# Graph network on one core: the top-p lists are taken from a scratch tile, and the mean of logits moves behind the register loads

## The reference, cut to what matters

```
for n in range(2):
    q = Xa @ W1.T @ W2.T;  k = Xa @ W3.T
    probs = softmax(q @ k.T)                  # 2048 x 2048
    # keep, row by row, the largest probabilities until their sum reaches 0.9
    A = probs * mask;  A = A / A.sum(-1)
    Xf = R @ Xf                               # R: adjacency with self loops, rows normed
    Xa = A @ Xa
    Z = Z + Xf @ U1[n].T + Xa @ U2[n].T
```

## Time and profile before

| | us |
|---|---|
| median of 3 runs (lowest, highest) | 1009.66 (1006.43, 1011.87) |
| the profiled execution | 1009.86 |
| its span from first to last instruction | 1008.1 |
| PE, DVE, ACT, POOL busy | 800.5, 664.4, 474.4, 69.2 |

### The profile page before, as it was taken

One profiled execution on the slowest core, in us unless ns is written; L12 is line 12 of the kernel. 1 busy time (PEld: TensorE's weight loads), 2 busy tenths in 40 slices (PEclk: granted clock), 3 DMA queues, 4 the chain that ended last, 5 costly groups with the idle time before them and its releaser, 6 DMA issues.

```text
span 1008.1 us, 11952 instructions
## 1 busy us (share of the span) xinstructions
PE 800.5 (79%) x3886; PEld 547.4 (54%) x3886; DVE 664.4 (66%) x2092; ACT 474.4 (47%) x945; POOL 69.2 (7%) x63
## 2 busy tenths in 40 slices
PE   4879984988888837568698688785698899994894
PEld 4844432756666726465375566565295485552342
DVE  5967868488597788832879878768777212235715
ACT  4886334336556483224535846856945141024111
POOL 0020001010000000000000000100001200013001
PEclk9889986988989977879697898989799999997898
DMA  9849502544004000000063400601342719200001
GB/s 332 333 167 429 212 10 84 170 164 136 33 1 168 1 1 2 0 2 1 2 213 120 167 1 1 225 2 53 135 167 85 283 52 413 86 1 0 1 0 42
DMA packets 20219, 108.23 MB, mean 107 GB/s; under 512 B 1824, under 2 KB 8752, under 8 KB 9776
## 3 DMA queue, kind: packets, MB, share of 16 engines
q1 hardware_dynamic: 18752, 106.77, 28.5%
q10 hardware_dynamic: 1392, 0.61, 0.2%
HBM read 88.23 MB, written 19.14 MB: 107 GB/s over the span
## 4 chain that ended last, share of the span: by engine, by line
PE 52%; DVE 22%; ACT 13%; issue 8%; POOL 2%; DMA 2%; DVEq 1%; POOLq 0%; SPq 0%; ACTq 0%
PE PS L795 11%; PE PS L600 6%; PE PS L664 6%; PE PS L534 6%; PE PS L717 5%; DVE AT L1513 4%; PE PS L864 4%; DVE mxv L1652 3%; DVE nd L1516 3%; ACT BC L1236 3%; PE PS L1045 3%; PE PS L1021 3%; ACT AT L1236 3%; DVE AT L2122 2%; PE PS L1051 2%
## 5 line engine op out<-in xcount | busy, mean ns | idle before, releaser
L1067 ACT ACTIVATE AT<-PS 128x512 f32<-128x512 f32 (+2 forms) x240 | 118.7, 560 | 132.6 <-PE PS L534 100.4
L534 PE MATMUL PS<-ident,AT 128*128 128x128 f32 x544 | 84.4, 290 | 47.9 <-DVE rS L2178 21.7
L1652 DVE TENSOR_REDUCE mxv<-PS 128x1 f32<-128x2048 f32 x32 | 73.2, 2288 | 68.7 <-PE PS L717 68.4
L717 PE MATMUL PS<-K,ST 64*128 64x512 f32 x256 | 87.0, 770 | 14.6 <-ACT EA L1204 7.8
L534 PEld LDWEIGHTS PS<-ident,AT 128*128 128x128 f32 x544 | 67.8, 150 | 56.3 <-DVE rS L2178 24.5
L2122 DVE MAX8 AT<-AT 128x8 f32<-128x256 f32 (+2 forms) x336 | 92.4, 347 | 0.7
L795 PE MATMUL PS<-hr,AT 128*128 128x128 f32 x512 | 71.7, 290 | 7.7 <-ACT AT L1067 6.9
L795 PE MATMUL PS<-AT 128*128 128x128 f32 x512 | 70.4, 286 | 7.9 <-ACT AT L1067 7.3
L795 PEld LDWEIGHTS PS<-hr,AT 128*128 128x128 f32 x512 | 65.4, 200 | 15.8 <-ACT AT L1067 10.5
L795 PEld LDWEIGHTS PS<-AT 128*128 128x128 f32 x512 | 64.1, 197 | 16.9 <-ACT AT L1067 10.9
L1067 ACT ACTIVATE ST<-PS 128x512 f32<-128x512 f32 (+3 forms) x43 | 23.9, 562 | 103.5 <-PE PS L1051 23.8
(11 more groups left out here) (297 smaller groups left out, 1369.4 us busy)
## 6 DMA issues: line engine op xcount, KB each, us to landing
AT<-keep_at SPq DMA_DIRECT2D x32, 1024.0 KB, 5.1
EA<-in_adj SPq DMA_DIRECT2D x20, 1024.0 KB, 6.6
keep_at<-AT SPq DMA_DIRECT2D x8, 2048.0 KB, 25.0
AT<-keep_at SPq DMA_DIRECT2D x8, 2048.0 KB, 12.4
AT<-in_adj SPq DMA_DIRECT2D x12, 1024.0 KB, 6.2
EA<-keep_degrees SPq DMA_DIRECT2D x1, 1024.0 KB, 6.6
keep_x<-K SPq DMA_DIRECT2D x4, 256.0 KB, 6.9
out<-EA SPq DMA_DIRECT2D x4, 256.0 KB, 2.3
```

The source lines that it names most:

```text
L534: return pe.transpose(dst, src, ident[0:p, 0:p])
L717: return pe.matmul(bank(to + n), ST[1][half_rows, k * P:(k + 1) * P], keys[half_rows, n * BK:(n + 1) * BK], start=True, stop=True)
L1067: return act.activation(dst, src, ACT.Copy)
L1652: v(dve.tensor_reduce(mxv[:, odd:odd + 1], PS[:, b:b + 4, :], AX.XY, ALU.max))
```

## The change

All of it is in VectorE's list and in where its tiles lie.

1. `under` writes to one scratch tile (row 10) for all four tiles, and `max` reads it; `cands[k]` holds kept values only. The wait for `e_turned` goes from `under` to the mask of the same tile. As the scratch tile is shared, `v.wait()` stands at the end of each tile's maxima.
2. In the groups that are not in BOTH, the maxima of logits of the next group move: `next_max(1)` from before the lists to behind the first `under`, `next_max(2)` and `next_max(3)` to the middle of the maxima of tiles 1 and 2.
3. In these groups `guess_gap` and `guess_first` of the next group move from tile 2's maxima to the first and third round of the list.
4. `logit_mean(gi + 2)` moves from before `crossing_checked` to behind `load_more`, in all groups that have it (gi = 0, 1, 4, 5).
5. `third_sum`, which is not called with SUMS = (1, 2), is removed. UNITS_IN stays.

```diff
+        scratch = row[:, 10, :]
+        def top_tile(step, m, k):
+            if m == 0 or step == 1:
+                return tops_of[step][m][:, k, :]
+            at = (1 + k // 2) * BK + k % 2 * SETS[0] * TOP
+            return row[:, 9, at:at + SETS[0] * TOP]
...
-            def under(w, E, bound, k, **kw):
-                w.put(stt(cands[k], E[:, k, :], bound[:, k:k + 1], ALU.is_lt, E[:, k, :], ALU.mult, **kw))
+            def under(w, to, E, bound, k, **kw):
+                w.put(stt(to, E[:, k, :], bound[:, k:k + 1], ALU.is_lt, E[:, k, :], ALU.mult, **kw))
...
+            def mask_tile(w, E, k):
+                w.put(stt(cands[k], E[:, k, :], s4[:, 0, k:k + 1], ALU.is_ge, E[:, k, :], ALU.mult,
+                          accum_out=Sk[:, k:k + 1]))
...
                 if gi in BOTH:
                     ...
                     first_sums(E, gi, early)
-                if SUMS[gi // NB] > 2:
-                    third_sum(E, gi, lambda: next_max(1))
-                else:
                     next_max(1)
...
                 for k in range(G):
-                    if gi > 0:
-                        dve.wait_ge(e_turned, 4 * (G * (gi - 1) + k + 1))
+                    under(v, scratch, E, q.th, k, accum_out=Lw[:, k:k + 1])
                     if gi not in BOTH and k == 0:
-                        next_max(2)
-                    under(v, E, q.th, k, accum_out=Lw[:, k:k + 1])
+                        next_max(1)
                     v.wait()
-                    if gi not in BOTH and k == 1:
-                        next_max(3)
...
                     for s in range(sets):
                         if s == sets // 2 and k < 2 and gi in BOTH:
                             next_max(k + 2)
-                        if s == sets // 2 and k == 2 and left > 0:
+                        if s == sets // 2 and k in (1, 2) and gi not in BOTH:
+                            next_max(k + 1)
+                        if s == sets // 2 and k == 2 and gi in BOTH:
                             guess_gap(gi + 1)
-                        v.put(dve.max(tops[0][:, k, s * TOP:(s + 1) * TOP], cands[k][:, ends[s]:ends[s + 1]]))
-                    if k == 2 and left > 0:
+                        v.put(dve.max(top_tile(step, 0, k)[:, s * TOP:(s + 1) * TOP], scratch[:, ends[s]:ends[s + 1]]))
+                    if k == 2 and gi in BOTH:
                         guess_first(gi + 1)
                         dve.sem_inc(th_ok, 1)
-                v.wait()
+                    v.wait()
...
                     for k in range(G):
                         v.put(dve.max(L[:, k, m * TOP:(m + 1) * TOP], top_tile(step, m % 2, k)))
                     v.wait()
-                if left > 1:
-                    logit_mean(gi + 2)
+                    if gi not in BOTH and left > 0:
+                        if m == 0:
+                            guess_gap(gi + 1)
+                        if m == 2:
+                            guess_first(gi + 1)
+                            dve.sem_inc(th_ok, 1)
                 crossing_checked(q)
                 doubtful()
...
                 load_more()
+                if left > 1:
+                    logit_mean(gi + 2)
                 if left > 0:
-                    masked(v, E)
+                    for k in range(G):
+                        if gi > 0:
+                            dve.wait_ge(e_turned, 4 * (G * (gi - 1) + k + 1))
+                        mask_tile(v, E, k)
+                else:
+                    dve.wait_ge(e_turned, 4 * G * gi)
```

More of the change, by code:

```diff
@@ L146, in gnn_kernel @@
         unit_st = [row[:, 8, 2 * BK + q * UNIT:2 * BK + (q + 1) * UNIT] for q in range(2)]
-        tops_at = [(row[:, 9, 0:BK], row[:, 10, 3 * BK:4 * BK]), (row[:, 9, BK:2 * BK], row[:, 9, 2 * BK:3 * BK])]
-        tops_of = [[half_[:, 0:sets * G * TOP].rearrange("p (k e) -> p k e", k=G) for half_ in pair]
-                   for pair, sets in zip(tops_at, SETS)]
+        scratch = row[:, 10, :]
+        tops_of = [[row[:, 9, m * BK:m * BK + SETS[step] * G * TOP].rearrange("p (k e) -> p k e", k=G)
+                    for m in ((0,), (1, 2))[step]] for step in range(STEPS)]
+        def top_tile(step, m, k):
[3 more added lines that the diff above has]
+            return row[:, 9, at:at + SETS[0] * TOP]
         set_ends = [[(m * N + sets // 2) // sets for m in range(sets + 1)] for sets in SETS]
@@ L1926, in shared_surplus @@
                 v(tt(q.fval[:, 0:G - 1], Fv[:, 0:G - 1], q.Tt[:, 0:G - 1], ALU.subtract))
[L1928 to L1944, removed]
-                    v.wait()
-                    shared_surplus(q, gi, 2)
-                else:
[L1948 to L1951, removed]
             def first_sums(E, gi, between):
@@ L2013, in crossing_checked @@
                 v.put(ts(s_(4), q.fval, 0.0, ALU.is_ge))
+            def mask_tile(w, E, k):
+                w.put(stt(cands[k], E[:, k, :], s4[:, 0, k:k + 1], ALU.is_ge, E[:, k, :], ALU.mult,
+                          accum_out=Sk[:, k:k + 1]))
             def masked(w, E):
                 for k in range(G):
-                    w.put(stt(cands[k], E[:, k, :], s4[:, 0, k:k + 1], ALU.is_ge, E[:, k, :], ALU.mult,
-                              accum_out=Sk[:, k:k + 1]))
+                    mask_tile(w, E, k)
             def ties(w):
@@ L2055, in surely @@
                 for k in range(G):
-                    under(w, E, hi, k)
+                    under(w, cands[k], E, hi, k)
                 w.wait()
@@ L2097, in group @@
                     first_sums(E, gi, early)
-                if SUMS[gi // NB] > 2:
-                    third_sum(E, gi, lambda: next_max(1))
-                else:
                     next_max(1)
-                tops, ends = tops_of[gi // NB], set_ends[gi // NB]
-                sets = SETS[gi // NB]
+                step = gi // NB
+                sets, ends = SETS[step], set_ends[step]
                 for k in range(G):
-                    if gi > 0:
-                        dve.wait_ge(e_turned, 4 * (G * (gi - 1) + k + 1))
+                    under(v, scratch, E, q.th, k, accum_out=Lw[:, k:k + 1])
                     if gi not in BOTH and k == 0:
-                        next_max(2)
-                    under(v, E, q.th, k, accum_out=Lw[:, k:k + 1])
+                        next_max(1)
                     v.wait()
-                    if gi not in BOTH and k == 1:
-                        next_max(3)
                     if k == G - 1:
@@ L2119, in group @@
                             next_max(k + 2)
-                        if s == sets // 2 and k == 2 and left > 0:
+                        if s == sets // 2 and k in (1, 2) and gi not in BOTH:
+                            next_max(k + 1)
+                        if s == sets // 2 and k == 2 and gi in BOTH:
                             guess_gap(gi + 1)
-                        v.put(dve.max(tops[0][:, k, s * TOP:(s + 1) * TOP], cands[k][:, ends[s]:ends[s + 1]]))
-                    if k == 2 and left > 0:
+                        v.put(dve.max(top_tile(step, 0, k)[:, s * TOP:(s + 1) * TOP], scratch[:, ends[s]:ends[s + 1]]))
+                    if k == 2 and gi in BOTH:
                         guess_first(gi + 1)
                         dve.sem_inc(th_ok, 1)
-                v.wait()
-                v.put(total(seen8, tops[0][:, :, TOP - 1:sets * TOP:TOP], ALU.max))
+                    v.wait()
+                v.put(total(seen8, tops_of[step][0][:, :, TOP - 1:sets * TOP:TOP], ALU.max))
                 for m in range(WINDOW // TOP):
@@ L2131, in group @@
                         for k in range(G):
-                            v.put(dve.match_replace(tops[m % 2][:, k, :], L[:, k, (m - 1) * TOP:m * TOP],
-                                                    tops[(m - 1) % 2][:, k, :], 0.0))
+                            v.put(dve.match_replace(top_tile(step, m % 2, k), L[:, k, (m - 1) * TOP:m * TOP],
+                                                    top_tile(step, (m - 1) % 2, k), 0.0))
                         v.wait()
                     for k in range(G):
-                        v.put(dve.max(L[:, k, m * TOP:(m + 1) * TOP], tops[m % 2][:, k, :]))
+                        v.put(dve.max(L[:, k, m * TOP:(m + 1) * TOP], top_tile(step, m % 2, k)))
                     v.wait()
-                if left > 1:
-                    logit_mean(gi + 2)
+                    if gi not in BOTH and left > 0:
[4 more added lines that the diff above has]
+                            dve.sem_inc(th_ok, 1)
                 crossing_checked(q)
```

## The result

The changed kernel takes 1028.15 us (median of 4 runs, 1027.90 to 1032.47); the kernel before took 1009.26 in the runs taken beside it. The ratio is 1.019, with a 95% interval of 1.016 to 1.022: slower, by 1.6 to 2.2%. The forecast was 1030.4. The profiled execution took 1028.08 us, 1026.3 of it span, against 1009.86 and 1008.1 before.

What follows compares the result with a forecast made beforehand. No engine's busy share bounds the kernel; each stage has its own last wait. 1009.86 - 7.1 (end of step 0) + 30.7 (step 1 delays) - 3.1 (last group) = 1030.4 us, range 1022 to 1041.

Steps and rivals of the forecast that it cites:

- The delay of step 1: Groups 4 and 5: the later logit_mean holds PE's fifth and seventh units, then ACT; exponentials 30.7 us late in all.
- the 9.42: Time of a late PE unit until ACT picks it up, taken from step 0; 7.66 us was the other bound.
- Group 0: Step 0: logit_mean right ahead of the mask starts the fifth unit 6.05 us late, carried on through group 1.
- The end of step 0: Groups 2 and 3: lists without waits and an earlier group 2 mask end step 0 7.1 us earlier.
- 342.85 + 33.1: Group 2: time of the second maximum plus the time to the mask, forecast at about 376.2.
- the tail: Group 3: what follows the last `max` up to the mask, 15.65 us, forecast to stay.
- The last group: Masks end before POOL's last two roots, which then run fast; 3.1 us won.
- the two large terms: The step 1 delay, +30.7 us, and the gain up to the end of step 0, -7.1 us.
- the mean slips past the loads: Rival: logit_mean does not wait out load_more's register loads, so the delays shrink; 1024.8 us, chance 0.07.
- nothing is won: Rival: no gain at the end of step 0 or in the last group, the loss alone; 1040.6 us, chance 0.13.
- one of the delays of step 1 is hidden: Rival: DVE reaches group 5's logit_mean before PE's logits, saving 15.3 us; 1015 us, chance 0.06.
- the late units cost nothing: Rival: nothing lost in groups 0, 4 and 5, so the kernel gets faster; 993.5 us, chance 0.06.

Runs made afterwards that it cites:

- E1: The changed kernel with logit_mean back at its old place before crossing_checked; 1001.83 us, ratio to before 0.9935.
- E2: The kernel before with only logit_mean moved behind load_more; 1055.23 us, ratio to before 1.0462.
- E5: The kernel before with the last group's masks held until ACT has scaled the last norm's rows; 1001.58 us, ratio to before 0.9954.
- E3: The changed kernel with logit_mean just ahead of load_more's register loads instead of behind them; 1025.60 us.
- E7: The changed kernel with maxima, thresholds and logit_mean in the order of before, leaving scratch tile and moved wait; 997.49 us, ratio to before 0.9912.
- E8: The changed kernel with logit_mean at its old place and maxima and thresholds in new order in step 0, old in step 1; 988.86 us, ratio to before 0.9833.
- E4: The changed kernel with logit_mean moved further, behind the four masks; 1066.4 us in a single run.

## Why the prediction was right

**The delay of step 1 (forecast +30.7, measured +32.7).** Its mechanism held in each row: `gs` behind the loads, PE standing 14.1 and 15.2 us, ACT 18 us, the second delay beginning from the first. E1 shows that moving `logit_mean` back takes the loss away, E2 that the move makes it without the rest of the change. The term is 2.0 us too small, mostly because a late unit takes longer than the 9.42 I had set as the upper bound: from PE's start to ACT's pickup 10.07, 10.27 and 10.32 us in groups 0, 4 and 5. (The row of ACT is at 240.04, not 240.01, so the unit of before took 9.45. The seventh unit of before did not take 7.66 us either: it ran from 628.05 to 636.75, 8.70 us at a granted clock of 0.87. The sum does not hang on that one, as it counts from the mean.)

**Group 0 (forecast +6.05, measured +6.6).** The same cause: 0.6 us for the unit (10.07 against 9.45 us). The 6 us are indeed carried through group 1 (-0.65), where the next `logit_mean` is covered.

**The end of step 0 (forecast -7.1 up to the end, measured -8.7).** Up to the `rS` of group 2 the sum is -1.8 where I had -0.9 to -1.1. My own terms give more: 342.85 + 33.1 is 375.95 and not 376.2, which is 1.4 us earlier than 377.32. The rest is the 0.65 us of group 1, to which I had given nothing, and 0.4 us more in group 2, less the 0.6 us of group 0. Four lists took 21.8 us (22 forecast), the tail 15.65, PE's idle time ahead of the turns 7.66 ("some 8"). Counted from the first mean on, group 3's mask is 7.85 us earlier; the other 0.86 lie behind it, in group 3's attention (34.84 us against 35.70), which I had taken as unchanged. PE's first turns of group 2 came 2.1 us later than before (386.14 and 386.97, each counted from its execution's first mean), where I had 2.4, and as forecast this did not reach group 3's mask.

**The last group (forecast -3.1, measured -3.3).** E5 shows cause and size apart from the rest of the change.

**What the sum lacked.** Group 6 lost 1.4 us although its exponentials stood as close as before. The loss lies right behind the last of them, where PE was busy for the same 7.59 us of a 10 us window but got through 51 matmuls instead of 66, at a granted clock of 0.83 instead of 1.00 (rows of the windows after and before, in the form that the last section explains):

```profile
706.00:716.00 10.00, 7.59 (x51) 7.12 (x50) 7.32 (x50) 5.71 (x19) 1.01 (x1) 0.83 0.04 12
```

```profile
686.00:696.00 10.00, 7.59 (x66) 7.12 (x64) 6.26 (x25) 5.96 (x19) 1.01 (x1) 1.00 0.10 28
```

The head of step 1 took 0.9 less; over the nine profiled executions it took 60.5 to 60.7 us in six and 61.4 to 61.5 in three, in no order that follows the edits. Start-up, ahead of all changed instructions, gave 2.9 us. From the first mean on the forecast is 0.6 us off (+20.5 and +21.1). That closeness is in part luck: errors of +2.0 and -1.6 us in the two large terms cancel in part, and single stages move by some 3 us between executions of the same instructions on PE and ACT (see the last section).

**The rivals.** That the mean slips past the loads is refuted by E3. That nothing is won is refuted by group 3's rows and by E7. That one of the delays of step 1 is hidden: both are there in the rows, 14.12 and 15.15 us. That the late units cost nothing is refuted by E1.

**What the prediction had not seen.** In step 1 the new order of maxima costs some 9 us of its own (E1 against E8), since there the threshold of the first list comes no earlier than the logits, and `under` only stands in the maximum's way; half of that is PE's lower clock behind the longer wait. In the changed kernel the late units hide this; it shows once they are mended.

## What to carry to other kernels

A tiny instruction that raises a semaphore is to be costed by who waits for the semaphore, on all engines, and not by its 0.16 us: here PE stood for 36 us (7.1 + 14.1 + 15.2) on account of it. Moving an instruction behind register loads moves it behind their whole length as well, here 1.8 to 2.0 us. An order that fills waits in one stage can stand in the way in another that has no such wait, so choose it by stage, and test each edit of a bundle alone: this bundle lost 1.9% and its parts without the moved mean, ordered by step, win 1.7%.

## What the runs showed of the hardware that was not expected

**The clock behind a long wait.** Windows of the changed kernel around the unit of group 4 (start and end, length, busy time and number of instructions of PE, PEld (TensorE's weight loads), DVE, ACT and POOL, granted TensorE clock, DMA share, GB/s):

```profile
545.00:554.30 9.30, 0.00 (x1) 0.00 (x1) 6.33 (x28) 1.44 (x2) 0.00 (x0) 0.50 0.00 0
554.30:556.00 1.70, 1.70 (x6) 1.52 (x7) 1.70 (x1) 0.00 (x0) 0.00 (x0) 0.50 0.09 19
556.00:558.00 2.00, 2.00 (x7) 1.64 (x7) 2.00 (x3) 0.00 (x0) 0.00 (x0) 0.50 0.00 0
558.00:560.00 2.00, 2.00 (x7) 1.62 (x6) 2.00 (x3) 0.00 (x0) 0.00 (x0) 0.58 0.02 4
560.00:562.00 2.00, 2.00 (x11) 1.74 (x11) 2.00 (x3) 0.00 (x0) 0.00 (x0) 1.00 0.00 0
```

PE had done nothing; the clock stood at 0.50 (1.2 GHz) while it waited and through the first half of the unit, and then at 1.00 (2.4 GHz). The same unit took 7.66 us at 1.00 and 10.27 here. The price does not follow the wait: 10.07 us behind 7.13 us of idle time, 10.32 behind 15.15, and about 9.2 in E4 behind 23.20. Nor does it need a long one: the unit that took 9.45 us before stood behind 0.85 us of idle time, at a mean granted clock of 0.81.

**Stages that differ between executions.** With the same instructions on PE and ACT group 5 took 77.69 us in the profiled execution of before and 74.3 to 74.4 in E5, E7 and E8. The rows of before and E5 show where: PE's granted clock. In both PE had stood still for the same 2.15 us; then before worked at 0.51 and 0.63 (609.7 to 613.7 us), E5 at 1.00 (607.8 to 611.8). Before the seventh unit it was again lower for longer, 0.50 from 624.3 to 630.0 us in before, and in E5 0.63, 0.50 and 0.86 from 620.4 to 625.7. The 17 runs of before that were taken beside these last three kernels lie in two clusters that the mean granted clock separates as well: 4 at 1000.8 to 1001.1 us with 0.901 to 0.905, and 13 at 1005.3 to 1009.6 us with 0.885 to 0.895. Why the clock is granted differently to the same instructions stays open. So does whether E5's edit shifts its runs to the lower cluster, or whether they only fell there: E5's edit is shown to be worth 3.2 us, not 6.8.
